# State mixer and factorised mixer of an early-fusion network as one stage, Silu as one ScalarE function, and a new order at the end of dispatch

## What is computed

```python
def _L1_attn_ref(x, W_in, conv_w, conv_b, W_xproj, A_log, D, W_out):
    x_proj, z = jnp.split(x @ W_in, 2, axis=-1)
    xc = conv over 4 taps of x_proj
    x_conv = silu(xc + conv_b)
    ssm = x_conv @ W_xproj
    delta, Bm, Cm = softplus(ssm[..., 0]), ssm[..., 1:17], ssm[..., 17:]
    h_mean = einsum('bld,bln->bdn', x_conv, delta[..., None] * Bm) / L
    y = einsum('bdn,bln->bld', h_mean, Cm) + D * x_conv
    return (y * silu(z)) @ W_out

def _L1_ffn_ref(x, proj, C1, Win1, Wout1, C2, Win2, Wout2):
    a = entmax15(layernorm(x @ proj))
    h = gelu((([x, 1] @ Win1) * (a @ C1)) @ Wout1.T)
    return (([h, 1] @ Win2) * (a @ C2)) @ Wout2.T

h = h + _L1_attn_ref(layernorm(h), ...)
h = h + _L1_ffn_ref(layernorm(h), ...)
```

## Time and profile before

| | |
|---|---|
| runs | 2786.33 us median of 3 (2784.88 to 2786.79) |
| profiled execution | 2791.91 us, span 2790.2 us |
| mean granted TensorE clock | 0.92 |
| busy PE | 2368.8 us (85%) |
| busy DVE | 2016.5 us (72%) |
| busy ACT | 1293.0 us (46%) |
| busy POOL | 842.1 us (30%) |

### The profile page before, as it was taken

The page is one execution under the profiler, slowest core; times in us unless marked ns, Lnnn a source line. Parts: engine busy times, 40 slices in busy tenths (PEclk is TensorE's granted clock), DMA queues, the critical chain, the costliest instruction groups (busy, mean ns, idle before and its releaser), DMA issues. The chain is left out here.

```text
span 2790.2 us, 53680 instructions
## 1 busy us (share of the span) xinstructions
PE 2368.8 (85%) x19286; PEld 1818.1 (65%) x19286; DVE 2016.5 (72%) x4822; ACT 1293.0 (46%) x3118; POOL 842.1 (30%) x698
## 2 busy tenths in 40 slices
PE   7999998997648998888888888977586938899798
PEld 6777776885536777667676777756464826677454
DVE  4889884333368898888888888997754447895673
ACT  0444442121356777767676677763121314353232
POOL 2111100000122333333333333335873067540110
PEclk9999998998569999999999999988688978899799
DMA  4221001011402222222211112223312932110000
GB/s 156 74 75 30 14 8 50 23 29 64 130 21 50 54 54 54 54 55 54 49 45 49 48 50 51 50 73 97 87 30 84 320 106 75 47 40 1 27 21 27
DMA packets 274614, 169.24 MB, mean 61 GB/s; under 512 B 182863, under 2 KB 250590, under 8 KB 274000
## 3 DMA queue, kind: packets, MB, share of 16 engines
q1 hardware_dynamic: 248221, 140.55, 17.7%
q0 software_dynamic: 26112, 25.03, 3.4%
HBM read 99.49 MB, written 73.45 MB: 62 GB/s over the span
## 5 line engine op out<-in xcount | busy, mean ns | idle before, releaser
L1405 POOL TENSOR_TENSOR qd<-decay,qm 114x456 f32<-114x456 f32 x128 | 163.6, 1297 | 557.5 <-DVE qm L1604 469.9
L2358 PEld LDWEIGHTS d_ps<-d_xT,resid 128*128 128x128 f32 x1024 | 196.7, 193 | 46.1 <-issue 28.9
L2358 PE MATMUL d_ps<-d_xT,resid 128*128 128x228 f32 x1024 | 215.3, 362 | 12.3 <-DMA d_xT<-normed_t 12.3
L1585 DVE TENSOR_TENSOR ue<-ue,elim_tmp 128x30 f32<-128x30 f32 (+14 forms) x480 | 210.4, 438 | 16.8
L2983 POOL DMA_INDIRECT s_eo<-rows_y,slots_all x128 | 156.4, 1222 | 147.1 <-POOLq L2795 109.1
L1647 DVE SCALAR_TENSOR_TENSOR y_v<-raw,taps,y_v 128x228 f32<-128x228 f32 x384 | 163.6, 499 | 48.4 <-ACT y_v L2025 48.4
L1583 DVE TENSOR_TENSOR elim_tmp<-ue 128x30 f32<-128x30 f32 (+14 forms) x480 | 178.7, 372 | 25.7 <-issue 10.3
L1987 ACT ACTIVATE decay<-d_ps,gates 114x114 f32<-114x114 f32 x512 | 138.0, 362 | 85.0 <-DVE nt L1617 52.4
L1647 DVE SCALAR_TENSOR_TENSOR y_qk<-raw,taps,y_qk 128x228 f32<-128x228 f32 x384 | 144.9, 452 | 23.3 <-ACT y_qk L2025 23.3
L2334 PE MATMUL d_ps<-y_qk 64*114 64x228 f32 x512 | 74.0, 412 | 99.2 <-DVE nt L1617 60.5
L1998 ACT ACTIVATE gl<-upto,gates 114x114 f32<-114x114 f32 x512 | 156.1, 392 | 0.5 <-PE d_ps L2346 0.2
(11 more groups left out here) (371 smaller groups left out, 5665.0 us busy)
## 6 DMA issues: line engine op xcount, KB each, us to landing
rows_x<-zero_row SPq DMA_DIRECT2D x4, 2048.0 KB
ue<-blocks_n SPq DMA_DIRECT2D x16, 512.0 KB, 5.2
blocks_u<-ue SPq DMA_DIRECT2D x16, 512.0 KB, 2.8
blocks_v<-on SPq DMA_DIRECT2D x16, 512.0 KB, 2.9
e_x<-rows_x SPq DMA_DIRECT2D x32, 256.0 KB, 4.5
e_gu<-L_ffn_w_gate_up SPq DMA_DIRECT2D x32, 256.0 KB, 4.5
rows_y<-e_y SPq DMA_DIRECT2D x32, 256.0 KB, 3.6
blocks_n<-nt SPq DMA_DIRECT2D x96, 64.0 KB
```

The lines of the kernel that those rows point to most:

```text
L1405: pool.tensor_tensor(qd[p.par][s][:, hs(u), :].rearrange("p (a o b) t -> p a o b t", o=2, b=2)[:, :, o], e[o][:, :, :].rearrange("p (a b) ...
L1585: step = dve.tensor_tensor(ue[:, 0:j, j + 1:], ue[:, 0:j, j + 1:], part, ALU.subtract)
L2358: last = pe.matmul(ps[:, f % 2, (t % 2) * W:(t % 2 + 1) * W], w_qkv[:, k, t * 128:(t + 1) * 128], xT[:, k, :], start=(k == 0), stop=(k == ...
```

## The change

The two mixers become one stage, `last_mixers`. Its semaphores are 32 and 29 and not 34 and 29 in two stages; `Core.end` clears all 61. The nine weight transfers of the factorised mixer are issued once the third turn of the state mixer is done. The last two groups of the state mixer are written out, with the factorised mixer's first norms, turns, logits and the first entmax put between their steps. Silu becomes one ScalarE function, in place for y and from PSUM for z, and the eight VectorE instructions a group and the halvings are gone. At the end of dispatch, the order of VectorE and TensorE is changed.

```diff
 # delta net, VectorE, last_turns
                     shared(2)
+                    normalise(7)
                     add_shared(1)
-                    normalise(7)
+                    choose(7)
                     shared(3)
+                    place(7)
                     add_shared(2)
-                    choose(7)
+                    share(7)
                     shared(4)
                     add_shared(3)
-                    place(7)
-                    share(7)
 # delta net, TensorE
                     outputs(r, 0)
                     outputs(r, 1)
+                    counts(5)
                     join(r, 2, False)
...
                     inverse(r, 3)
-                    counts(5)
...
                     turn(7)
+                    gate_logits(7)
                     gate_up(3)
+                    counts(7)
                     down(2)
-                    gate_logits(7)
                     gate_up(4)
                     down(3)
-                    counts(7)
 # last_mixers, SyncE, behind the state mixer's weights
                 c.clear_old(sp)
+                sp.wait_ge(s_t, 6)
+                for dst, src in (nine weights of the factorised mixer):
+                    sp.dma_start(dst, src).then_inc(fw_in, 16)
 # ScalarE
-                    act.activation(th[:, t, :], y[j % 2][:, t, :], ACT.Tanh, scale=0.5).then_inc(sth, 1)
+                    act.activation(y[j % 2][:, t, :], y[j % 2][:, t, :], ACT.Silu).then_inc(syy, 1)
-                    act.activation(sz[j % 2][:, t, :], ps[:, t, 0:L], ACT.Tanh, scale=0.5).then_inc(sthz, 1)
+                    act.activation(sz[j % 2][:, t, :], ps[:, t, 0:L], ACT.Silu).then_inc(ssz, 1)
 # ScalarE, behind softplus(7), the last of its loop over groups
+                f_xT_read(0)
+                bcT_read(G - 1)
+                f_xT_read(1)
+                aT_read(0)
 # VectorE, silu
-                    dve.scalar_tensor_tensor(sz[j % 2][:, t, :], sz[j % 2][:, t, :], 1.0, ps[:, t, 0:L], ALU.add, ALU.mult).then_inc(ssz, 1)
-                    dve.scalar_tensor_tensor(y[j % 2][:, t, :], th[:, t, :], 1.0, y[j % 2][:, t, :], ALU.add, ALU.mult).then_inc(syy, 1)
 # VectorE, groups 6 and 7 and the border (skipped and gated of the four tiles written as one)
+                conv(7); f_statistics(0); mixing_read(6); skipped, gated (6, 0); f_scale(0)
+                skipped, gated (6, 1 to 2); f_statistics(1); skipped, gated (6, 3)
+                step_sizes(7); f_scale(1); step_gates(7); sort_logits(0)
+                result(6); f_statistics(2); mixing_read(7); moments(0)
+                skipped, gated (7, 0 to 3); threshold(0); f_scale(2); result(7)
+                sort_logits(1); dve.wait_ge(fw_in, 16 * FW)
                 for i in range(G):
                     first_gate(i)
-                    if i == 0: sort_logits(1); moments(1)
+                    if i == 0: moments(1)
                     threshold(i + 1); norm(i + 3); sort_logits(i + 2)
                     second_gate(i); moments(i + 2); result(i)
 # TensorE, group 6 from state_inputs(7) on, and group 7
+                        pe.wait_ge(fw_in, 16 * FW)
+                        f_turn(0)
+                        project_out(6, (0, 1))
+                        logits(0)
+                        project_out(6, (2, 3))
+                turn_bc(7); mixing(7); f_turn(1); mixed(7); logits(1)
+                project_out(7)
                 gates_first(0)
```

More of the change, by code:

```diff
@@ L3160, in _ @@
                         norm_scale(n)
+                dve.wait_ge(f_init, GS + 1)
+                fch(dve.reciprocal(rk[:, :, :], ks[:, :, :]))
+                j = G - 2
+                conv(j + 1)
+                f_statistics(0)
+                mixing_read(j)
+                skipped(j, 0)
+                gated(j, 0)
+                f_scale(0)
+                skipped(j, 1)
+                skipped(j, 2)
+                gated(j, 1)
+                gated(j, 2)
+                f_statistics(1)
+                skipped(j, 3)
+                gated(j, 3)
+                step_sizes(j + 1)
+                f_scale(1)
+                step_gates(j + 1)
+                sort_logits(0)
+                result(j)
+                f_statistics(2)
+                j = G - 1
+                mixing_read(j)
+                moments(0)
+                skipped(j, 0)
+                skipped(j, 1)
+                gated(j, 0)
+                gated(j, 1)
+                skipped(j, 2)
+                skipped(j, 3)
+                gated(j, 2)
+                gated(j, 3)
+                threshold(0)
+                f_scale(2)
+                result(j)
+                sort_logits(1)
+                dve.wait_ge(fw_in, 16 * FW)
+                for i in range(G):
+                    first_gate(i)
+                    if i == 0:
+                        moments(1)
+                    if i + 1 < G:
+                        threshold(i + 1)
+                    if i + 3 < G:
+                        f_statistics(i + 3)
+                        f_scale(i + 3)
+                    if i + 2 < G:
+                        sort_logits(i + 2)
+                    second_gate(i)
+                    if i + 2 < G:
+                        moments(i + 2)
+                    f_result(i)
+                fch.sync()
                 ch.sync()
@@ L3248, in _ @@
                         first_tap(j + 2)
+                f_xT_read(0)
+                bcT_read(G - 1)
+                f_xT_read(1)
+                aT_read(0)
+                for i in range(G):
+                    for n in range(2):
+                        act.wait_ge(fg_mm, 2 * i + n + 1)
+                        if i:
+                            act.wait_ge(fz2, i)
+                        act.copy(g[:, n, :], ps[:, 5 + n, 0:L]).then_inc(fg, 1)
+                    if i + 2 < G:
+                        f_xT_read(i + 2)
+                    for t in range(OT):
+                        act.wait_ge(h_mm, OT * i + t + 1)
+                        if i and t == 0:
+                            act.wait_ge(z2_mm, i)
+                        act.activation(hT[:, t, :], ps[:, 4 + t % 4, 0:L], ACT.Gelu).then_inc(fh, 1)
+                    if i + 1 < G:
+                        aT_read(i + 1)
             @block.tensor
@@ L3325, in mixed, with project_out @@
                         last.then_inc(y_mm, 1)
-                def project_out(j):
+                def project_out(j, samples=range(GS)):
                     pe.wait_ge(syz, 4 * j + 4)
-                    for s in range(GS):
+                    for s in samples:
                         for t in range(CT):
@@ L3682, in _ @@
+                turn_bc(G - 1)
+                mixing(G - 1)
+                f_turn(1)
+                mixed(G - 1)
                 logits(1)
+                project_out(G - 1)
                 gates_first(0)
                 for i in range(G):
-                    gates(i)
+                    f_gates(i)
                     if i + 2 < G:
-                        turn(i + 2)
+                        f_turn(i + 2)
                     pe.wait_ge(fz1, i + 1)
@@ L3717, in _, with mixed @@
                             last.then_inc(o_mm, 1)
-def mixed(c, rows_x, hid, xts):
+def mixed(c, rows_x, hid, xts, out):
     nc = c.nc
@@ L3745, in program @@
         c.resid = c.arena[0:S, :, :]
-        mixed(c, rows_x, hid, xts)
-        c.stage(factorised_mlp, out)
+        mixed(c, rows_x, hid, xts, out)
         c.end()
```

595 lines of the change are left out of this document (256 added, 339 removed).

## The result

The changed kernel takes 2751.7 us, the median of four runs (2749.87 to 2756.1), against 2786.56 for the kernel before beside it: a ratio of 0.9861, 95% interval 0.9849 to 0.9873. The medians differ by 34.9 us, and the ratio makes 38.7 of 2786.56. The forecast was 2752.0. The profiled execution has a span of 2750.0 against 2790.2, 40.2 less. A table of stretches, each taken from one trace of either kernel, says where the difference lies. A border is counted here from the end of the last state inputs (line L3296 before, L3544 after) to the start of out(1).

A forecast was written before the change was run, and what follows sets the result against it. TensorE was taken as full in steady groups, with time to win at the border between the mixers. Border -32.0, dispatch -4.3 and end +2.0 sum to -34.3, from 2786.3 to 2752.0 us; range 2741 to 2764.

The forecast's parts named there:

- The border, -32.0: From the state mixer to out(1) of the factorised mixer: interleaving saves 32.0 us, a start-up gain of 0.9 included.
- The three steps inside: At the border: h(0) 20.5 us earlier, out(0) 5.2 more, out(1) 6.3 more.
- the first two steps: h(0) 20.5 us earlier by work moved ahead; out(0) 5.2 more, one sort having left the stretch from h(0).
- Cover: Group 0's moments and threshold hide behind project_out(7), else 6.5 us; weight transfers hide in the state stage, else 1.79.
- Silu: State groups: Silu takes Tanh's 0.58 us, removes 5.0 of VectorE work a group, adds table loads; steady groups unchanged.
- The start-up was sized -0.9: First state groups: POOL's gathers set the pace, so Silu gains only 0.9 us; bounds -18.8 and +3 x 1.28.
- Dispatch, -4.3: End of dispatch: the new order makes slot(7) earlier, cutting POOL's wait before its last 16 scatters; 4.3 us saved.
- counts(5): In dispatch, moved behind outputs(r,1): frees nothing, POOL having other work there; 0, between -1 and +1 us.
- The end, +2.0: Behind the output's landing SyncE clears 61 semaphores in place of 29: 2.0 us more, bounds 0 to 4.
- the first rival: At the border TensorE's clock falls again ahead of h(0), losing 6.3 us: 2758; chance 0.20.
- VectorE was not the bound: Rival at the border: pieces moved onto VectorE delay project_out(7), 18.8 us less gain, 2771; chance 0.09.
- Silu was not dear: Rival from conv to tokens in every group: Silu at 2.0 us makes the kernel slower, 2807; chance 0.03.

The follow-up runs named there:

- the serial kernel: Changed kernel, one stage and early weights kept, with the last two state groups and first factorised groups in the old order, one behind the other: 2776.72 us.
- the kernel with Tanh: Changed kernel with Tanh on ScalarE and eight VectorE instructions a group again in place of Silu: 2759.86 us.
- Silu alone: The kernel before with only the Silu part of the change: 2786.14 us beside 2789.36, ratio 0.9987.
- the early clearing: State mixer's 32 semaphores cleared while SyncE waits for the third group's output; run on the changed kernel together with five border moves: 2745.74 us.
- the kernel with the late sort: Changed kernel with the sort of group 1 put back behind the first gate of group 0: 2756.56 us.
- that of the five moves: Changed kernel with five pieces of work reordered or split in the border, and the state mixer's 32 semaphores cleared early: 2745.74 us.
- without its Exp the kernel: Changed kernel with the Exp of softplus left out, one table load less a group: 2752.23 us.

## Why the prediction was right

By its own steps, in the order of its sum:

- **The border, -32.0 with the start-up in it.** Measured -31.2 for the border and -3.2 for start-up and steady groups. The three steps inside hold: h(0) 20.3 earlier, measured from the last state inputs (59.36 to 39.06), where the working gave 19.6 (its 20.5 less the 0.9 of the start-up); out(0) 4.6 more (5.2 forecast); out(1) 6.3 more (6.3 forecast). The shift of project_out(7) was 5.3 where the working, from the same point, gave 4.5, and its matmuls then took 7.16 in place of 8.57, which the forecast did not have. One sum on the way does not come out: from the read of the state inputs to the sort, 3.4, 0.9 and 1.7 make 6.0, while its two times, 2552.20 less 0.9 and 2558.4, are 7.1 apart, so 1.1 stands there without a term. Measured are 6.4 (2541.65 to 2548.09). By its own terms the forecast would have been 2750.9. Behind the sort two sizes were off: from mixed(7) to project_out(7) are 8.9 where the working kept 7.7, since mixed(7) took 7.02, at a granted clock of 0.52, and project_out(7) then took 1.4 less than in the working. That these two nearly cancel is luck. The reason behind the first two steps stood its test: one sort moved back into VectorE's row of work cost 8.1 in the border. In the changed kernel that row and TensorE's own are within 0.8 us of each other at out(0): the second gate ends at 2596.99, and out(0) starts at 2597.77 behind matmuls.
- **Cover.** Threshold(0) ran beside project_out(7), from 2566.08 to 2570.44, as forecast, and the weights never showed. The interleaving as a whole is 26.3 of the 31.2. The one stage with its weights, for which the prediction named the 1.79 of the logits' wait alone, shows 4.9 in the serial kernel.
- **Silu.** Its duration, its loads and the steady groups came as forecast. The start-up was sized -0.9 and gave -2.8: that step took POOL's gathers for the pace, while the kernel with Tanh is 3.0 slower there. Since TensorE's clock differs between these traces in the same stretch, and Silu alone gave 0.6, no run here shows what the term should have been. The forecast also costed the eight instructions at nothing in groups 6 and 7, and there the kernel with Tanh loses 3.1 us of the border, through a wait for VectorE and the lower clock behind it, and, with group 6 itself, part of 1.9 more. The sum was spared that, since the change has both; a forecast for the interleaving alone would have been too good by that much.
- **Dispatch, -4.3.** Measured -4.2, and no gain at POOL from counts(5), for the reason given: POOL has the `ms` instruction waiting there.
- **The end, +2.0.** Measured 2.0, and taken back by the early clearing.
- **The rivals.** The clock was lower in h(0), as the first rival had it, and cost 1.7 there in place of 6.3; of these 0.8 at most reached out(0), since the second gate would have held it that long anyway, and out(0) started without an idle time. VectorE was not the bound, but within reach of it, as the kernel with Tanh shows. Silu was not dear. No run here shows a drain behind a table load: in softplus(7) the first load ends at 2543.68 and Exp starts within 0.02 of it, the second ends at 2545.20 and Ln starts 0.01 behind it. The 1.4 that the Trainium skill, page "ScalarE: Activation LUTs", section "What ACT_TABLE_LOAD costs", would have added did not come. Exp and Ln loaded a table each, eight times, so the set with both functions that the Trainium skill names on that page, section "Table sets: the hidden batching unit", was not what this program loaded.

The agreement of 2752.0 with 2751.7 is closer than the working can claim, and so in part luck: the stretches give -36.5 where the sum had -34.3, with 1.9 of the difference in the start-up, and a median of this kernel moves by some us with a stretch ahead of dispatch.

## What to carry to other kernels

At the border of two stages, write down which engine's row of work sets the first large matmul behind it, and move pieces of that row into time in which that engine idles ahead of the border; joining the stages without that gave 4.9 of 31 us here. Ask what makes room for the moved pieces: an edit that buys nothing in steady groups can be what lets them fit. Where runs spread by more than the effect, compare stretches between two instructions of the traces, which repeated to 0.1 us for the same kernel. Then look at TensorE's clock inside them: between kernels the same eight matmul tiles took 6.36 or 8.05 where no edit had touched them.

## What the runs showed of the hardware

- TensorE's lower clock at the border wanders. h(0) took 8.08 behind an idle time of 2.22 and h(6) and h(7) 8.06 and 8.05 behind 0.72 in the changed kernel, and 6.28 when that time was filled. But with the same 0.72 ahead of them h(6) and h(7) took 6.36 in the kernel with the late sort, as did h(7) in that of the five moves, and without its Exp the kernel had f_turn(0) at 1.76 in place of 0.98 with no idle time ahead. What decides is open; time won in one piece of a border was in part lost in the next.
- A float32 matmul of 128x456 stands in the trace as two records and takes 0.80, as h's eight tiles in 6.31 also say; I had counted one record.
- The instructions ahead of dispatch's end, the same but for the place of counts(5), ended between 2043.5 and 2053.7 us in the traces, which no edit here explains.
